# A perceiver layer on one core: each pass's scatter adds to residual rows written to the result, and the passes' probabilities and tokens come from one product

## The reference

```python
x = x + xattn(layernorm(x), ctx, ctx, Wq, bq, Wk, bk, Wv, bv)   # softmax(q k^T) v
x = x + dss(layernorm(x), D, Lambda, log_dt, W)                 # FFT convolution with a made kernel, + u * D
x = x + moe(layernorm(x), w_gate, b_gate, W1, b1, W2, b2)
# moe, on 512 tokens, 8 experts, 512 -> 2048 -> 512:
probs = softmax(xn @ w_gate + b_gate); route_p = max(probs); e = argmax(probs)
out = (relu(xn @ W1[e] + b1[e]) @ W2[e] + b2[e]) * route_p
```

## Time and profile before

| | |
|---|---|
| median of the runs | 382.45 us |
| profiled execution | 383.73 us |
| its span | 381.8 us |
| TensorE busy | 322.7 us (85%) |
| VectorE, ScalarE, GpSimd busy | 212.0, 143.8, 38.4 us |
| read from HBM | 90.94 MB |

### The profile page before, as it was taken

One profiled execution on the slowest core, in us unless ns is written; L12 is line 12 of the kernel. 1 busy time (PEld: TensorE's weight loads), 2 busy tenths in 40 slices (PEclk: granted clock), 3 DMA queues, 4 the chain that ended last, 5 costly groups with the idle time before them and its releaser, 6 DMA issues.

```text
span 381.8 us, 8325 instructions
## 1 busy us (share of the span) xinstructions
PE 322.7 (85%) x3134; PEld 190.6 (50%) x3134; DVE 212.0 (56%) x423; ACT 143.8 (38%) x262; POOL 38.4 (10%) x66
## 2 busy tenths in 40 slices
PE   0899999999999799695869986779999679979790
PEld 0674675758886445463334443434454434434340
DVE  1688867999667479555244444433554333244443
ACT  4959987978122002202123232222222222213121
POOL 3140000000000001003102110001111011111111
PEclk9999999999999999869899999998999998989896
DMA  7999966198552990004960069999004999999920
GB/s 173 371 371 349 416 257 227 24 382 300 186 210 60 413 387 29 8 2 170 381 227 22 21 231 401 385 397 388 28 14 150 400 390 391 395 384 401 388 91 1
DMA packets 35032, 93.75 MB, mean 246 GB/s; under 512 B 3166, under 2 KB 5854, under 8 KB 33474
## 3 DMA queue, kind: packets, MB, share of 16 engines
q1 hardware_dynamic: 30866, 88.54, 62.4%
q0 software_dynamic: 1600, 3.56, 3.4%
q10 hardware_dynamic: 2544, 1.36, 1.4%
HBM read 90.94 MB, written 2.56 MB: 245 GB/s over the span
## 4 chain that ended last, share of the span: by engine, by line
PE 56%; DMA 21%; DVE 12%; issue 7%; POOL 2%; DVEq 1%; ACT 1%; POOLq 1%; SPq 0%; ACTq 0%
DMA out<-small,cols 15%; PE bank L1482 8%; PE bank L1277 7%; PE bank L1258 7%; PE bank L1455 6%; DVE tab L1127 5%; PE bank L1287 4%; PE bank L1210 3%; DMA ring<-in_wq_t 2%; DMA sorted_rows<-x_ext,icols 2%; DVE small L1127 2%; PE bank L1238 2%; PE bank L1323 2%; PE bank L1467 2%; PE bank L1266 2%
## 5 line engine op out<-in xcount | busy, mean ns | idle before, releaser
L1482 PE MATMUL bank<-ring,hbuf 128*32 128x512 f32 x496 | 66.4, 638 | 16.3 <-DVE hbuf L1113 14.8
L1455 PE MATMUL bank<-ring,small 128*32 128x256 f32 x1184 | 73.5, 386 | 7.1 <-ACT small L704 6.6
L1455 PEld LDWEIGHTS bank<-ring,small 128*32 128x32 f32 x1184 | 43.9, 112 | 34.3 <-issue 10.9
L1121 DVE COPY cols<-tab 32x1 uint32<-32x1 uint32 x20 | 2.8, 141 | 83.4 <-DMA out<-small,cols 75.9
L682 ACT ACTIVATE bank<-bank 32x512 f32<-32x512 f32 x60 | 33.7, 562 | 36.3 <-PE bank L1482 35.2
L1127 DVE SCALAR_TENSOR_TENSOR tab<-bank,tab 32x512 f32<-32x512 f32 x60 | 44.0, 733 | 3.4 <-ACT bank L682 0.8
L1482 PEld LDWEIGHTS bank<-ring,hbuf 128*32 128x32 f32 x496 | 15.5, 115 | 51.5 <-issue 51.3
L704 ACT ACTIVATE small<-late 128x128 f32 x19 | 5.9, 310 | 70.5 <-issue 44.4
L1258 PE MATMUL bank<-ring 128*128 128x512 f32 x64 | 29.7, 594 | 0.0
L688 ACT ACTIVATE hbuf<-bank 128x256 f32<-128x256 f32 x38 | 14.6, 383 | 38.2 <-PE bank L1455 38.2
L1277 PE MATMUL bank<-ring 128*128 128x256 f32 x128 | 28.4, 379 | 0.0
(11 more groups left out here) (187 smaller groups left out, 439.6 us busy)
## 6 DMA issues: line engine op xcount, KB each, us to landing
ring<-in_w SPq DMA_DIRECT2D x30, 2048.0 KB, 15.7
ring<-in_ctx_turned SPq DMA_DIRECT2D x4, 2048.0 KB, 11.7
ring<-in_ctx SPq DMA_DIRECT2D x4, 2048.0 KB, 12.7
work<-in_w SPq DMA_DIRECT2D x2, 2048.0 KB, 18.1
tab<-sorted_rows ACTq DMA_DIRECT2D x19, 64.2 KB, 4.9
ring<-in_wq_t SPq DMA_DIRECT2D x4, 256.0 KB, 9.3
x_ext<-in_x SPq DMA_DIRECT2D x4, 256.0 KB, 9.5
x_ext<-in_bv POOLq DMA_DIRECT2D x4, 256.0 KB, 12.3
```

The costliest lines, as they stand in the source:

```text
L1455: ins = pe.matmul(bank[j * TW:(j + 1) * TW, H_BANK[s], 0:HN], xw[:, d, :], first_layer(e, s)[:, d, j * HN:(j + 1) * HN], start=d == 0, sto ...
L1482: ins = pe.matmul(bank[j * TW:(j + 1) * TW, Y_BANK, :], h_t[s][:, c, j, :], second_layer(e, s)[:, HC * j + c, :], start=s == 0 and c == 0, ...
```

## The change

1. The residual rows, with the bias added, are written plainly to the result: four DMAs in SyncE's queue ahead of unit 8. GpSimd's scatter of a pass has `compute_op=ALU.add` and adds 32 rows to them. The sums have no residual in them, so the first is only a product. `sorted_rows`, its scatters and the loads per pass go.
2. Tokens and probabilities of all passes lie in `small`, one column for a pass. They come from one product of TensorE (the fill "meta"): VectorE makes, for every token, a one-hot row of its place in its window (`row_hot`) and its probability and token number in the column of its window (`pairs`).
3. The copy of a pass's tokens, with its wait for the last scatter, stands ahead of the fourth sum, and that sum stands behind the second half's rectification.
4. ScalarE no longer waits for the bias products ahead of the first pass; the waits for these banks are with the moved parts. VectorE's bias additions stand between and behind its two sorted copies.
5. One filler ahead of the last gate product and three behind it. The pad rows at the start of GpSimd's queue are replaced by two small DMAs that only count `rows_sent` up.

The core of the diff:

```diff
         b1_sb = small[:, 0:NE * MCH].rearrange("p (e c) -> p e c", e=NE)
         xw = small[:, NE * MCH:NE * MCH + DCH * TW].rearrange("p (c n) -> p c n", c=DCH)
         y_out = small[0:TW, 512:1024]
-        x_rows_w = tab[0:TW, P:P + D + 2]
-        y_sum = x_rows_w[:, 0:D]
+        y_sum = tab[0:TW, P:P + D]
+        meta_prob = small[0:TW, 256:256 + MAXW + 1]
+        meta_token = small[0:TW, 256 + MAXW + 1:256 + 2 * (MAXW + 1)].bitcast(U32)
...
@@ -455,6 +465,11 @@
         if j == NB:
             for b in range(NB):
                 sp.dma_start(b2_sb[b * TW:b * TW + NE, :], b2).then_inc(b2_loaded, 16)
+        if j == 8:
+            for b in range(NB):
+                after_read(sp, ("b2", b))
+            for b in range(NB):
+                sp.dma_start(out[b * P:(b + 1) * P, :], x_sb[:, b, :]).then_inc(rows_written, 16)
         load_unit(j)
     sp.wait_ge(windows_ready, 1)
...
@@ -668,17 +683,11 @@
         sorted_tokens(act, c, lambda dst, src: act.activation(dst, src, ACT.Identity))
-    def load_rows(first_row, w):
-        act.wait_ge(y_summed, CT * w + 2 * CT)
-        act.wait_ge(sorted_sent, 16 * NB)
-        act.wait_ge(rows_sent, 32)
-        act.dma_start(x_rows_w, sorted_rows[bass.ds(first_row, TW), :]).then_inc(x_rows_loaded, 16)
     def output_moved(w, k):
         act.wait_ge(stages_done, UNITS * w + UNITS)
         act.wait_ge(y_summed, CT * w + k + 1)
...
@@ -691,8 +700,6 @@
     for c in range(DCH):
         after_read(act, ("xs", c))
     act.wait_ge(pad_ready, 1)
-    for b in range(NB):
-        after_read(act, ("b2", b))
     for e in range(NE):
...
@@ -1076,32 +1081,64 @@
     link(dve.tensor_reduce(cum9, cum_prod, AX, ALU.add))
     dve.tensor_copy(win_i, cum9).then_inc(windows_ready, 1)
     dve.tensor_copy(off_i, off9[:, 0:NE]).then_inc(windows_ready, 1)
-    dve.tensor_copy(row_i, slot).then_inc(rows_ready, 1)
-    dve.tensor_copy(token, table("token")).then_inc(rows_ready, 1)
-    one_ahead = UNITS * [stages_done] + CT * [y_summed] + [x_rows_loaded]
+    one_ahead = UNITS * [stages_done] + CT * [y_summed]
     for i, s in enumerate(one_ahead):
         dve.memset(spare[:, i:i + 1], 0.0).then_inc(s, 1)
     dve.wait_ge(lexp_ready, 1)
     link(dve.tensor_reduce(psum_e, lexp, AX, ALU.add))
     dve.reciprocal(prob, psum_e).then_inc(prob_ready, 1)
+    def per_w(v):
+        return v.unsqueeze(2).to_broadcast([P, NB, MAXW + 1])
+    link(dve.scalar_tensor_tensor(out=cum9[:, 0:NE], in0=cum9[:, 0:NE], scalar=TW, in1=off9[:, 0:NE],
+                                  op0=ALU.mult, op1=ALU.subtract))
+    link(dve.tensor_tensor(ahead_e, hot, cum9[:, 0:NE].unsqueeze(1).to_broadcast([P, NB, NE]), ALU.mult))
+    link(dve.tensor_reduce(ahead, ahead_e, AX, ALU.add))
+    link(dve.scalar_tensor_tensor(out=ahead, in0=ahead, scalar=TW, in1=slot, op0=ALU.add, op1=ALU.add))
+    link(dve.scalar_tensor_tensor(out=from_window,
+                                  in0=table("iota")[:, 0:MAXW + 1].unsqueeze(1).to_broadcast([P, NB, MAXW + 1]),
+                                  scalar=-float(TW), in1=per_w(ahead), op0=ALU.mult, op1=ALU.add))
+    link(dve.tensor_scalar(in_window, from_window, float(TW), None, ALU.is_lt))
+    link(dve.scalar_tensor_tensor(out=in_window, in0=from_window, scalar=0.0, in1=in_window,
+                                  op0=ALU.is_ge, op1=ALU.mult))
+    link(dve.tensor_tensor(row_in, in_window, from_window, ALU.mult))
+    link(dve.tensor_reduce(row_of, row_in, AX, ALU.add))
+    dve.tensor_tensor(row_hot, table("iota")[:, 0:TW].unsqueeze(1).to_broadcast([P, NB, TW]),
+                      row_of.unsqueeze(2).to_broadcast([P, NB, TW]), ALU.is_equal).then_inc(meta_ready, 1)
+    dve.wait_ge(prob_ready, 1)
+    dve.tensor_tensor(pairs[:, :, 0, :], in_window, per_w(prob), ALU.mult).then_inc(meta_ready, 1)
+    dve.tensor_tensor(pairs[:, :, 1, :], in_window, per_w(table("token")), ALU.mult).then_inc(meta_ready, 1)
     after_fill(dve, ("b2", NB - 1))
     dve.memset(xs_t[:, :, NB * P:NB * P + TW], 0.0).then_inc(pad_ready, 1)
     dve.wait_ge(windows_ready, 2)
     bounds = [dve.value_load(win_i[0:1, e:e + 1], min_val=0, max_val=MAXW) for e in range(2)]
-    for c in range(1, DCH, 2):
-        sorted_tokens(dve, c, dve.tensor_copy)
-    dve.wait_ge(prob_ready, 1)
-    for b in range(NB):
+    def output_bias(b):
         src = may_read(dve, ("b2", b))
         did_read(dve.scalar_tensor_tensor(out=x_sb[:, b, :], in0=src, scalar=x_ext[:, b, D:D + 1], in1=x_sb[:, b, :],
                                           op0=ALU.mult, op1=ALU.add), ("b2", b))
+    output_bias(2)
+    sorted_tokens(dve, 1, dve.tensor_copy)
+    output_bias(0)
+    sorted_tokens(dve, 3, dve.tensor_copy)
+    output_bias(1)
+    output_bias(3)
+    src = may_read(dve, ("meta",))
+    dve.tensor_copy(meta_prob, src[0:TW, 0:MAXW + 1])
+    did_read(dve.tensor_scalar(meta_token, src[0:TW, MAXW + 1:2 * (MAXW + 1)], float(NO_TOKEN), None, ALU.add),
+             ("meta",))
     dve.wait_ge(bias_loaded, 16)
     after_read(dve, ("xs", 0))
...
@@ -1115,17 +1152,17 @@
     def output_summed(w, k):
         dve.wait_ge(y_summed, CT * w + CT + k)
+        weight = meta_prob[:, bass.ds(w, 1)]
         if k == 0:
-            dve.wait_ge(x_rows_loaded, 16 * w + 1)
+            dve.wait_ge(stages_done, UNITS * w + UNITS)
+            dve.tensor_scalar(y_sum, bank[0:TW, Y_BANK, :], weight, None, ALU.mult).then_inc(y_summed, 1)
+            return
+        if k == CT - 1:
             dve.wait_ge(rows_sent, 16 * w + 16)
-            dve.tensor_copy(out_token, x_rows_w[:, D + 1:D + 2].bitcast(U32))
-            dve.wait_ge(stages_done, UNITS * w + UNITS)
-            src = bank[0:TW, Y_BANK, :]
-        else:
-            dve.wait_ge(y_part_ready, (CT - 1) * w + k)
-            src = bank[0:TW, PART_BANK[k - 1], :]
-        dve.scalar_tensor_tensor(out=y_out if k == CT - 1 else y_sum, in0=src, scalar=x_rows_w[:, D:D + 1],
-                                 in1=y_sum, op0=ALU.mult, op1=ALU.add).then_inc(y_summed, 1)
+            dve.tensor_copy(out_token, meta_token[:, bass.ds(w, 1)])
+        dve.wait_ge(y_part_ready, (CT - 1) * w + k)
+        dve.scalar_tensor_tensor(out=y_out if k == CT - 1 else y_sum, in0=bank[0:TW, PART_BANK[k - 1], :],
+                                 scalar=weight, in1=y_sum, op0=ALU.mult, op1=ALU.add).then_inc(y_summed, 1)
...
@@ -1136,8 +1173,8 @@
                 output_summed(w, 1)
                 hidden_relu(e, w, 0)
                 output_summed(w, 2)
+                hidden_relu(e, w, 1)
                 output_summed(w, 3)
-                hidden_relu(e, w, 1)
     for k in range(CT):
...
@@ -1170,13 +1202,7 @@
     for k in range(1, 2 * NB + 1):
         inverse_root(k + 1)
-    pool.wait_ge(rows_ready, 2)
-    pool.wait_ge(prob_ready, 1)
-    for b in range(NB):
-        after_read(pool, ("b2", b))
-        pool.indirect_dma_start(sorted_rows, bass.IndirectOffsetOnAxis(ap=row_i[:, b:b + 1], axis=0),
-                                x_ext[:, b, :], None).then_inc(sorted_sent, 16)
-    pool.wait_ge(sorted_sent, 16 * NB)
+    pool.wait_ge(rows_written, 16 * NB)
     pool.wait_ge(windows_ready, 2)
     windows = pool.value_load(win_i[0:1, NE:NE + 1], min_val=0, max_val=MAXW)
...
@@ -1187,7 +1213,7 @@
         pool.wait_ge(send_turn, w + 1)
         pool.tensor_tensor(rstd, m_half, m_half, ALU.mult).then_inc(send_turn, 1)
         pool.indirect_dma_start(out, bass.IndirectOffsetOnAxis(ap=out_token, axis=0), y_out, None,
-                                bounds_check=NB * LQ - 1, oob_is_err=False).then_inc(rows_sent, 16)
+                                bounds_check=NB * LQ - 1, oob_is_err=False, compute_op=ALU.add).then_inc(rows_sent, 16)
     pool.wait_ge(rows_sent, 16 * windows + 32)
...
@@ -1404,7 +1430,9 @@
     after_read(pe, ("lg", 1))
     keep_warm(2, tab[:, 0:2 * P])
     turn_gate_rows(3)
+    keep_warm(1, tab[:, 0:2 * P])
     gate(3)
+    keep_warm(3, tab[:, 0:2 * P])
...
@@ -1441,6 +1469,14 @@
     for batches in (range(0, 2), range(2, NB)):
         for c in range(DCH):
             sorting(c, batches)
+    dst = may_fill(pe, ("meta",))
+    pe.wait_ge(meta_ready, 3)
+    for b in range(NB):
+        ins = pe.matmul(dst[0:TW, 0:2 * (MAXW + 1)], row_hot[:, b, :], pairs[:, b].rearrange("p k w -> p (k w)"),
+                        start=b == 0, stop=b == NB - 1)
+    did_fill(ins, ("meta",))
```

More of the change, by code:

```diff
@@ L48 @@
 EPS = 1e-5
+NO_TOKEN = 1024
 ROUND = 1.5 * 2.0 ** 23
@@ L94 @@
           *(((T1, T2, O_BANK, T0)[b], ("b2", b)) for b in range(NB))]
-FILLS += [(S_BANK[c], ("xs", c)) for c in range(DCH)]
+FILLS += [(S_BANK[c], ("xs", c)) for c in range(DCH)] + [(O_BANK, ("meta",))]
 FILL_NO = {}
@@ L105, in perceiver_layer @@
                     w_gate, b_gate, w1, b1, w2, b2, times, tables, out):
-    sorted_rows = nc.dram_tensor("sorted_rows", ((NB + 1) * P, D + 2), F32, kind="Internal").ap()
+    sends_ahead = nc.dram_tensor("sends_ahead", (2, NB), F32, kind="Internal").ap()
```

(29 more changed lines are left out.)

4 lines of the change are left out of this document (removed).

## The result

The changed kernel takes 364.75 us in the median of four runs (363.14 to 365.18), against 382.7 for the kernel before on the same chip: a ratio of 0.9523 (95% interval 0.9482 to 0.9563). 361 was forecast, with 357 to 369 as the range. The profiled execution took 365.18 us, its span 363.4.

What follows compares the result with a forecast made beforehand. Bound: the scatter's landing in weight traffic (pitch 11.04 us, TensorE 8.57), then the weight stream. Pass 0 at 175.2, unit 19 at 272.2, TensorE's end 350.0 against 372.5, span 360.6: 361 us, range 357 to 369.

Steps and rivals of the forecast that it cites:

- The scatter's ring: Expert stage: with the wait at the fourth sum, the ring from scatter to scatter is 7.7 us, under TensorE's 8.57.
- Adding, e = 1: Scatter in the expert stage: adding lengthens each landing by e, taken as 1 us, bounds 0 and 3.4; ring 8.7 us.
- Rivals B and C: Scatter's landing binds: B, ring 10.1 us, 367 us, chance 0.18; C, landing over 9.4 us, 380 to 393 us, 0.05.
- The weight stream sets the end: Last part: unit 31 lands 75.8 us after unit 19's issue, 2.0 us of matmuls follow, TensorE ends at 350.0.
- Rival D: Last stage bound by weights alone, gaining nothing; result reads slowing the stream 3% would cost 2 us, 363; chance 0.04.
- Before the first pass: Ahead of pass 0: ScalarE's shorter wait and the fillers bring its start to 175.2; TensorE's new product takes under 1 us.
- Fillers: Around the last gate product: four fillers in idle time hold the clock, gaining 1.9 us, pass 0 at 175.2.
- rival A: Ahead of pass 0: the clock falls anyway, pass 0 starts at 177.1, 363 us; chance 0.20.
- ScalarE's wait: Ahead of pass 0: waiting for the sorted copies alone, not all four bias products, gains 2.6 us, start 177.1.
- Pad rows: Kernel start: removing them from GpSimd's queue, with VectorE's wait on them, changes nothing.
- The sum: Whole kernel: pass 0 at 175.2, unit 19 at 272.2, TensorE's end 350.0, tail 9.8 us, span 360.6, time 361 us.

Runs made afterwards that it cites:

- e2: Changed kernel with the token copy and its scatter wait back ahead of the first sum, fourth sum ahead of the second rectification: 382.85 us, ratio 0.9969.
- e5: Changed kernel with a plain scatter in place of the adding one: 364.54 us, ratio 0.9511.
- e4: Kernel before with only the token copy, its scatter wait and the fourth sum moved behind the second rectification: 393.19 us, ratio 1.0245.
- e6: Changed kernel with TensorE's nine bounds loads kept together but ahead of the new product, not behind it: 358.88 us, ratio 0.9364.
- e1: Changed kernel with TensorE loading two bounds ahead of the expert loop and each further one at its expert: 359.16 us, ratio 0.9357.
- e8: Changed kernel with two bounds loaded ahead of the loop, the rest in it, and without the four new fillers: 359.59 us, ratio 0.9361.
- e7: Changed kernel with ScalarE's wait for all four bias products ahead of pass 0 put back: 363.51 us, ratio 0.9461.
- e10: Changed kernel with bounds loaded in the loop and ScalarE's wait for the bias products put back: 361.19 us, ratio 0.9409.
- e9: Changed kernel with the pad rows' two starting DMAs, their fills and VectorE's wait put back, the two small DMAs removed: 366.39 us, ratio 0.9556.

## Why the prediction was right, point by point

- **The scatter's ring.** Right in mechanism and size. Adding scatters under traffic landed in 6.0 us on average, so the ring is 7.8 us and stays under TensorE's 8.57. The copy of the tokens waited for a scatter once, for 0.3 us. With the wait back in its old place (e2) some 17 of the 18 us are lost.
- **Adding, e = 1.** The bounds were 0 and 3.4; measured 0.6 (e5). The choice of the row with as many rows carried was the right one. The 2 us which the Trainium skill ("DMA: Bandwidth & Descriptors", section "Latency and other measured facts") gives for an HBM access at high load did not appear on top: the slowest landing stayed at 6.9 us with or without adding. Rivals B and C fall with it. Some of their figures were slightly off by their own numbers (4.4 us for 4.6, 15.9 for 15.5; the slowest bias DMA took 17.2 us, not 15), which moves neither time.
- **The weight stream sets the end.** Right, with the size 2.3 us too long: unit 19 to the landing of unit 31 took 73.5 us (277.79 to 351.3), forecast 75.8; 1.9 us of products behind it, as forecast. I took the length over from the kernel before, where ScalarE's reloads were in the same traffic. The time goes with them: 75.7 and 75.1 us in the kernel before and e4, which reload, 73.2 to 73.7 in all the others, e2 with its old pitch among them. The reloads themselves moved 0.4 MB, some 1 us of that stream; where the rest comes from is open. Rival D's slower stream did not come. A microsecond ahead of pass 11 counts in full, as e6 shows: unit 19 is issued 7.75 us sooner and the span is 8.0 us shorter.
- **Before the first pass: the step that failed.** "I take 1.9 us of gain, start 175.2" left TensorE's own queue out. I had counted VectorE's two loads of bounds, and TensorE's product as "under 1 us", but not what stands behind the product: nine loads, 7.5 us. The rows' DMAs, which I had put at nothing, are under way during the slowest of these; no run tells whether they cause it. In the kernel before they were over at 177.1, 2.6 us ahead of pass 0, and so hidden. The start came at 178.5, 3.3 us late, and the idle time brought the clock down for pass 0, 10.91 us against 8.57: 2.3 us. Together 5.6, which is how late unit 19 was (277.8 against 272.2). e1 and e6 show it: with the loads out of the way it goes out at 270. VectorE, which I took to be the late one, was not: its last sorted copy was done at 172.0, where I had 174.6, and ScalarE's columns were ready at 172.9.
- **Fillers.** The clock held where I said it would, and rival A is out. But they are worth nothing measurable: in the changed kernel the loads hide them, and with the loads moved (e1 against e8) the low clock in pass 0 took half of the 3.1 us back by unit 19.
- **ScalarE's wait.** Sized at 2.6 us; worth 0 in the changed kernel (e7), since the loads end later. Without them it moves pass 0's start by 1.3 us and unit 19 by nothing (e1 and e10), and the times don't tell the two apart.
- **Pad rows.** "Nothing" was probably wrong by 1 us: I looked at who waited for them and not at the first weights' DMAs, which take 8.5 us to land beside them (e9) and 6.9 without.
- **The sum.** Span 360.6 forecast + 5.6 (pass 0) - 2.3 (stream) - 0.8 (the clock fell in pass 16, ahead of a wait for weights, and cost nothing at the end) + 0.3 (tail 10.2 us) = 363.4, as measured. That the forecast came so near is in part luck: the stream and the clock gave back 3.1 of the 5.6 us that pass 0 had cost. A stream of 8 units is 48 us by the sum I wrote, not 47; nothing hangs on it. The pad rows' microsecond is inside the first of these.

## What to carry to other kernels

A wait in a loop costs the ring that it closes, so draw the ring from release to release before moving it: the same move saved 17 us where nothing else was in the ring and lost 9 us where a reload was. When an instruction gets a new wait, read on in its engine's program for the register loads behind it; they are not counted as busy, and the idle time shows as "issue", but the view of their source line gives their times. When one stream sets the end, work ahead of its start is worth its full time. Work beside it costs nothing only as long as it keeps up: in e2 TensorE ended 8.7 us after the last weights had landed, in the changed kernel 2.0.
